# A fused cross-attention and FFN kernel: the first three row tiles projected by a W_in that is not centred, and the mask steps three tiles later

## The chip, the cores and the metric

The kernel runs on one core of one Trainium2 chip. The metric is the device time in microseconds; three runs of the kernel before gave 839.51, 840.79 and 841.10 us, median 840.79. The engines are TensorE (PE in the profile; PEld is its weight load), VectorE (DVE), ScalarE (ACT), GpSimd (POOL) and SyncE (SP, which issues most DMAs). Each works through its own queue of instructions in order and waits on semaphores.

## The reference, cut to what matters

```
x: 4096 x 512, ctx: 3202 x 1024, mask: 3202 (int32)
h    = rmsnorm(layernorm(x), g_res) @ W_in + b_in          # 512 -> 512
s    = linear scan over ctx rows of rmsnorm(ctx, g_init)[:, :512]
plug = clip(cumsum(boundary_mask) - 1, 0, 3201), where boundary_mask is 1 at cumsum(mask) - 1
x    = x + h + s[plug]
x    = x + gelu(layernorm(x) @ W1 + b1) @ W2 + b2          # 512 -> 2048 -> 512
```

All in float32. The kernel keeps this precision by splitting each factor in a high part (float32r, one pass of TensorE) and a low part, and adding three products: high by high, high by low, low by high.

The layernorm in front of W_in subtracts each row's mean and divides by a deviation; the RMS norm that follows only changes the divisor. So h is a row's scale `ra` times (x - mean) @ (g_res * W_in). Subtracting the mean of x is the same as taking from each column of g_res * W_in its mean over the 512 rows: that is the *centred* W_in of the kernel before.

## The kernel before

The 4096 rows of x are 32 tiles of 128 rows (`NT`), in groups of `TI` = 4. A first stage, about the first 122 us, makes x1 = x + h for all tiles; a second one, the rest of the span, does the FFN for 8 groups. The change touches the first stage, and there the order of work is written out by hand, one queue per engine: whatever stands in a `for t in range(NT)` loop under `if t == ...` is issued at that step, and waits where it stands.

What one tile t needs: `load_tile` (SyncE) brings it to `xa(t)`; TensorE's `transpose_first` turns it into a PSUM bank `first_bank[t % 3]`; ScalarE's `tile_high` writes h_hi; VectorE's `tile_low` subtracts it from the bank to h_lo; TensorE's `project` adds 4 x 3 matmuls into `p_bank[t % 3]`; VectorE's `tile_stats` (bn_stats, bn_aggr), or ScalarE's for the tiles of `ON_ACT`, gives mean and variance; GpSimd's `scales` turns the variances to `ra`; VectorE's `tile_add` (L1047) writes ra * bank + x.

W_in comes in four slabs of 128 rows. ScalarE scales each by g_res (win_g, L724). TensorE multiplies the raw slabs with g_wide, g_res spread over 128 columns (`sum_w_in`, L853), so that acc[3] holds the column sums in every partition. VectorE centres each slab (`centre_w_in`, L1139), ScalarE writes its high part, VectorE the low part of slabs 0 and 1 (`low_w_in`, L1144), GpSimd that of slabs 2 and 3 (L570). Only then do the projections of tiles 0, 1 and 2 run.

In the same loop VectorE works through the mask: `mask_parts` at t = 1, a product on TensorE (`mask_totals`, t = 4), `mask_positions` (5), `mask_carries` (6), `mask_places` (7), `mask_rows` (8), the one-hots `one_hots_q` (9), `one_hots_p` (10 and 14); TensorE counts with them at t = 16 (`count_positions`). These are chains of small operations of 26 to 78 elements per partition, each waiting for the one before. And two blocks of the context scan: ScalarE's `squares`, GpSimd's multiplication by g_init (L544, from t = 5, behind the wait for the last of four small loads that ScalarE issues, L739 and L740), ScalarE's `scale_rows`, VectorE's `scan_row` (L1053: t = 12, 13 for block 0, t = 15, 16 for block 1), then TensorE's `carry`: block 0 at t = 15, block 1 at t = 18 (L890, one product of band and the last scanned row into acc[3]), and `add_carry` on VectorE (L1071). GpSimd adds b_in to the first group's rows from t = 14 (L552).

## Time and profile before

| | |
|---|---|
| median of 3 runs | 840.79 us |
| the profiled execution | 838.94 us, its span 837.2 us |
| TensorE busy | 825.7 us (99%), 3770 matmuls |
| VectorE, ScalarE, GpSimd busy | 317.4, 288.0, 255.9 us |
| end of the first stage's projections | about 122 us |

The profile shows one execution. A busy time is the union of an engine's instructions; behind a group of instructions it says how long the engine was idle ahead of it and what released it. The chain of waits is followed backwards from the last instruction, at each step to what released it.

### The profile page before, as it was taken

The page shows a single profiled execution, that of the slowest core. Times are in us where ns is not written, and L with a number is a line of the kernel's source. Part 1 is how long each engine was busy: PE and PEld are TensorE (multiplying, and loading weights), DVE is VectorE, ACT ScalarE, POOL GpSimd, SP SyncE. Part 2 cuts the span into 40 slices and gives each one's busy share as a digit, 9 for nine tenths or more (in the row PEclk, how much of TensorE's full clock was granted, in tenths as well). Part 3 has the DMA queues.
Part 4 walks back from the last instruction along what each step waited for, and adds up shares of the span by engine and source line. Part 5 has one row for each costly group of instructions (what it writes and reads, how often), then busy time and mean ns, then how long its engine had stood idle before and what let it go on. Part 6 is the DMA issues. An engine that isn't in the chain of part 4 may idle for free.

```text
span 837.2 us, 10780 instructions
## 1 busy us (share of the span) xinstructions
PE 825.7 (99%) x3770; PEld 680.7 (81%) x3770; DVE 317.4 (38%) x521; ACT 288.0 (34%) x522; POOL 255.9 (31%) x236
## 2 busy tenths in 40 slices
PE   7998999999999999999999999999999999999998
PEld 5887888788888888888888888888888888888886
DVE  6899762664241333223332424142113311242112
ACT  5664336532622253223522262222222322222221
POOL 2272547950443026301631062303400250002000
PEclk9999999999999999999999999999999999999999
DMA  9868885252226022511234113302300240010001
GB/s 242 255 174 272 232 270 195 75 148 40 76 88 174 0 76 75 155 31 60 78 106 92 45 41 125 50 0 101 51 0 1 83 68 0 0 51 0 1 1 50
DMA packets 37328, 74.96 MB, mean 90 GB/s; under 512 B 6176, under 2 KB 6176, under 8 KB 35536
## 3 DMA queue, kind: packets, MB, share of 16 engines
q1 hardware_dynamic: 28324, 62.81, 23.2%
q0 software_dynamic: 4608, 8.39, 6.4%
q10 hardware_dynamic: 4368, 3.42, 1.4%
q8 instruction: 14, 0.23, 0.1%
q14 instruction: 14, 0.11, 0.0%
HBM read 47.87 MB, written 22.84 MB: 84 GB/s over the span
## 4 chain that ended last, share of the span: by engine, by line
PE 85%; POOL 4%; DVE 4%; DMA 2%; issue 1%; SPq 1%; ACT 1%; ACTq 0%; DVEq 0%; POOLq 0%
PE acc L860 14%; PE acc L858 14%; PE acc L859 14%; PE h_bank L858 13%; PE h_bank L860 13%; PE h_bank L859 13%; DMA xa_odd<-in_x_dram 2%; PE t_bank L917 2%; POOL w_lo L525 1%; POOL x_cur L623 1%; POOL cl L544 1%; POOL w_lo L531 1%; DVE h_lo L1039 1%; DVE st_a L1034 1%; SPq L348 0%
## 5 line engine op out<-in xcount | busy, mean ns | idle before, releaser
L1264 DVE TENSOR_TENSOR h_lo<-g_f,h_hi 128x512 fp32r<-128x512 f32 x128 | 99.7, 779 | 432.1 <-ACT g_f L795 427.1
L793 ACT ACTIVATE h_hi<-h_bank,b_c 128x512 fp32r<-128x512 f32 x128 | 88.1, 689 | 430.9 <-PE h_bank L860 426.0
L858 PE MATMUL h_bank<-xt_hi,w_hi 128*128 128x512 f32 x512 | 199.9, 390 | 0.6 <-POOL w_lo L525 0.6
L858 PE MATMUL acc<-w_hi,h_hi 128*128 128x512 f32 x512 | 199.8, 390 | 0.0
L860 PE MATMUL h_bank<-xt_hi,w_lo 128*128 128x512 f32 x512 | 199.3, 389 | 0.0
L859 PE MATMUL h_bank<-xt_lo,w_hi 128*128 128x512 f32 x512 | 199.3, 389 | 0.0
L860 PE MATMUL acc<-w_hi,h_lo 128*128 128x512 f32 x512 | 199.2, 389 | 0.0
L859 PE MATMUL acc<-w_lo,h_hi 128*128 128x512 f32 x512 | 199.2, 389 | 0.0
L858 PEld LDWEIGHTS h_bank<-xt_hi,w_hi 128*128 128x128 f32 x512 | 96.1, 188 | 20.7 <-issue 1.0
L860 PEld LDWEIGHTS h_bank<-xt_hi,w_lo 128*128 128x128 f32 x512 | 96.1, 188 | 20.0
L860 PEld LDWEIGHTS acc<-w_hi,h_lo 128*128 128x128 f32 x512 | 96.1, 188 | 20.0
L859 PEld LDWEIGHTS h_bank<-xt_lo,w_hi 128*128 128x128 f32 x512 | 96.1, 188 | 19.7
L859 PEld LDWEIGHTS acc<-w_lo,h_hi 128*128 128x128 f32 x512 | 96.1, 188 | 19.7
L858 PEld LDWEIGHTS acc<-w_hi,h_hi 128*128 128x128 f32 x512 | 96.1, 188 | 19.7
L795 ACT ACTIVATE g_f<-h_bank,b_c 128x512 f32<-128x512 f32 x128 | 87.4, 683 | 0.3 <-DVE h_lo L1264 0.3
L557 POOL DMA_INDIRECT x_next<-scan_table,idx x32 | 50.9, 1591 | 69.7 <-DMA scan_table<-cl 59.7
L623 POOL TENSOR_TENSOR x_cur<-x_next,b_b 128x512 f32<-128x512 f32 x32 | 45.0, 1436 | 58.7 <-DMA out_dram<-x_cur 58.4
L544 POOL TENSOR_TENSOR cl<-cl,g_init_b 128x512 f32<-128x512 f32 x24 | 31.9, 1334 | 97.7 <-ACT ch L704 91.8
L552 POOL TENSOR_TENSOR x_next<-x_next,b_in_b 128x512 f32<-128x512 f32 x32 | 45.4, 1418 | 33.5 <-DMA x_next<-x_part 30.2
L562 POOL TENSOR_SCALAR va_b<-mv_b 128x4 f32<-128x4 f32 x8 | 1.6, 197 | 175.8 <-DVE mv_b L1170 175.8
L858 PE MATMUL acc<-win_hi,h_hi 128*128 128x512 f32 x88 | 37.2, 422 | 2.1 <-DVE win_lo L1144 1.9
L860 PE MATMUL acc<-win_hi,h_lo 128*128 128x512 f32 x88 | 34.6, 393 | 0.0
(164 smaller groups left out, 689.3 us busy)
## 6 DMA issues: line engine op xcount, KB each, us to landing
out_dram<-x_cur SPq DMA_DIRECT2D x32, 256.0 KB, 2.1
x_next<-x_part SPq DMA_DIRECT2D x7, 1024.0 KB, 5.0
w_raw<-in_L_ffn_w_dram SPq DMA_DIRECT2D x6, 1024.0 KB, 9.0
scan_table<-cl SPq DMA_DIRECT2D x6, 896.0 KB
ch<-in_ctx_dram SPq DMA_DIRECT2D x20, 256.0 KB
cl<-in_ctx_dram SPq DMA_DIRECT2D x5, 1024.0 KB
xa_odd<-in_x_dram SPq DMA_DIRECT2D x16, 256.0 KB, 6.2
x_part<-xa_odd SPq DMA_DIRECT2D x16, 256.0 KB, 3.8
```

The costliest lines, as they stand in the source:

```text
L525: pool.tensor_tensor(w_lo[:, k, r], w_raw[:, k, r], w_hi[:, k, r].bitcast(F32), ALU.subtract).then_inc(w1_ready, 1)
L544: pool.tensor_tensor(rows[:, j, :], rows[:, j, :], g_init_b[:], ALU.mult).then_inc(g_scaled, 1)
L552: step(pool.tensor_tensor(x_next[:, i, :], x_next[:, i, :], b_in_b[:], ALU.add))
L557: pool.indirect_dma_start(x_next[:, i, :], None, rows, bass.IndirectOffsetOnAxis(ap=idx[:, i:i + 1].bitcast(U32), axis=0), compute_op=ALU. ...
L623: ins = pool.tensor_tensor(x_cur[:, i, :], x_next[:, i, :], b2_b[:], ALU.add)
L793: act.activation(h_hi[:, m % HB, :], h_bank[m % 2][:], ACT.Gelu, bias=b1_c[:, m:m + 1])
L795: act.activation(g_f32[:], h_bank[m % 2][:], ACT.Gelu, bias=b1_c[:, m:m + 1]).then_inc(gelu_done, 1)
L858: nc.tensor.matmul(dst, a_hi, b_hi, start=first, stop=False)
L859: nc.tensor.matmul(dst, a_hi, b_lo, start=False, stop=False)
L860: return nc.tensor.matmul(dst, a_lo, b_hi, start=False, stop=final)
L917: ins = nc.tensor.transpose(t_bank[i % 2][:, k * P:(k + 1) * P], n_rows[:, i, k * P:(k + 1) * P], ident[:])
L1264: dve.tensor_tensor(h_lo[:, m % HB, :], g_f32[:], h_hi[:, m % HB, :].bitcast(F32), ALU.subtract).then_inc(h_split, 1)
```

## The change

For tiles 0, 1 and 2 the product is taken with g_res * W_in as it is, split into `first_hi` (ScalarE) and `first_lo` (VectorE), in two places of memory that are free at this time. The part of the mean is put in on VectorE: `fix_tile` writes x + neg_sums * mean_ra into the result's rows, with neg_sums the negative column sums and mean_ra = mean * ra (GpSimd), and `tile_add` then adds ra * bank to that. The column sums come from one product with ones, of the four scaled slabs added up on GpSimd (`add_w_in`); ScalarE copies them out of the bank as neg_sums. Tile 3 is the first that uses the centred W_in; all four of its low parts are made on VectorE. Tiles 3 and 4 are summed in acc[3] and h_bank[0], which no tile used so far (`sums_bank`), so that they wait for no `tile_add`. The transpositions and high and low parts of tiles 4 and 5 move ahead of the loop. W_in's slabs 1 and 2 are loaded by ScalarE's queue, x tiles 0, 1, 2 by SyncE's. The warm-up is 10 instead of 14 transpositions. `mask_parts` and `mask_totals` are three steps later, the steps of the mask behind them two.

```diff
-WARM = 14
+WARM = 10
+RAW = 3
+        first_hi = place("first_hi", [P, K, D], F32R, offset=w_hi_at + 2 * WC * 4)
+        first_lo = place("first_lo", [P, K, D], F32R, offset=w_hi_at + 3 * WC * 4)
+        win_sum = ch[:, 0, :]
+        def sums_bank(t):
+            return {3: acc[3], 4: h_bank[0]}[t] if t in (3, 4) else p_bank[(t + 2 * (t < 3)) % 3]
# SyncE
-            for k in range(K):
+            for t, k in ((0, 0), (1, 3)):
+                sp.dma_start(xa(t), x_v[0, :, t, :]).then_inc(xa_loaded[t], 16)
                 sp.dma_start(win_raw[:, k, :], win_v[:, k, :]).then_inc(win_loaded[k], 16)
+            sp.dma_start(xa(2), x_v[0, :, 2, :]).then_inc(xa_loaded[2], 16)
# GpSimd
-            for k in (2, 3):
-                pool.wait_ge(win_hi_done, k + 1)
-                pool.tensor_tensor(win_lo[:, k, :], win_raw[:, k, :], win_hi[:, k, :].bitcast(F32),
-                                   ALU.subtract).then_inc(win_lo_late, 1)
+            def add_w_in(k):
+                pool.wait_ge(win_scaled, k + 1)
+                src = win_g[:, 0, :] if k == 1 else win_sum
+                ins = pool.tensor_tensor(win_sum, src, win_g[:, k, :], ALU.add)
...
+            def mean_scales(t0, n):
+                pool.wait_ge(ra_ready, t0 + n)
+                u = slice(t0, t0 + n)
+                pool.tensor_tensor(mean_ra[:, u], mv_a[:, u, 0], ra[:, u], ALU.mult).then_inc(mean_ra_ready, n)
+            add_w_in(1)
+            add_w_in(2)
+            add_w_in(3)
             scales(0, 2)
+            mean_scales(0, 2)
             scales(2, 2)
+            mean_scales(2, 1)
# ScalarE
-            for t in range(2):
-                act.dma_start(xa(t), x_v[0, :, t, :]).then_inc(xa_loaded[t], 16)
+            for k in (1, 2):
+                act.dma_start(win_raw[:, k, :], win_v[:, k, :]).then_inc(win_loaded[k], 16)
+            def high_first(k):
+                act.wait_ge(win_loaded[k], 16)
+                act.activation(first_hi[:, k, :], win_raw[:, k, :], ACT.Copy, scale=g_res_c[:, k:k + 1]).then_inc(first_hi_done, 1)
+            high_first(0)
             tile_high(0)
+            high_first(1)
+            scale_w_in(0)
+            scale_w_in(1)
+            tile_high(1)
+            high_first(2)
+            scale_w_in(2)
+            high_first(3)
+            scale_w_in(3)
+            tile_high(2)
+            act.wait_ge(win_summed, 1)
+            act.activation(neg_sums[:], acc[3][:], ACT.Copy, scale=-1.0).then_inc(neg_sums_made, 1)
             high_w_in(0)
-            tile_high(1)
-            high_w_in(1)
-            tile_high(2)
-            high_w_in(2)
-            high_w_in(3)
             tile_high(3)
+            for k in range(1, K):
+                high_w_in(k)
+            tile_high(4)
+            tile_high(5)
# TensorE
-            def sum_w_in(k):
-                pe.wait_ge(g_made, k + 1)
-                pe.wait_ge(win_loaded[k], 16)
-                ins = nc.tensor.matmul(acc[3][:], g_wide[:, k, :], win_raw[:, k, :], start=(k == 0), stop=(k == K - 1))
+            def sum_w_in():
+                pe.wait_ge(win_added, 1)
+                nc.tensor.matmul(acc[3][:], ones[:], win_sum, start=True, stop=True).then_inc(win_summed, 1)
             def project(t):
                 pe.wait_ge(x_lo, t + 1)
-                if t >= 3:
-                    pe.wait_ge(acc_read, t - 2)
+                if t == RAW:
+                    pe.wait_ge(neg_sums_made, 1)
+                if t >= 5:
+                    pe.wait_ge(acc_read, t - 4 if t < 8 else t - 2)
                 for k in range(K):
+                    if t == RAW:
+                        pe.wait_ge(win_lo_done, k + 1)
-                if t == 4:
+                if t == 7:
+                    pe.wait_ge(acc_read, 5)
                     mask_totals()
# VectorE
+            def fix_tile(t):
+                dve.wait_ge(mean_ra_ready, t + 1)
+                ins = dve.scalar_tensor_tensor(x1(t), neg_sums[:], mean_ra[:, t:t + 1], xa(t), ALU.mult, ALU.add)
+                fixed.append(own.inc(ins))
             def centre_w_in(k):
-                    dve.wait_ge(win_summed, 1)
+                    dve.wait_ge(neg_sums_made, 1)
-                dve.scalar_tensor_tensor(win_raw[:, k, :], acc[3][:], -1.0 / D, win_g[:, k, :], ALU.mult, ALU.add)\
+                dve.scalar_tensor_tensor(win_raw[:, k, :], neg_sums[:], 1.0 / D, win_g[:, k, :], ALU.mult, ALU.add)\
+            def low_first(k):
+                dve.wait_ge(first_hi_done, k + 1)
+                dve.scalar_tensor_tensor(first_lo[:, k, :], win_raw[:, k, :], g_res_c[:, k:k + 1],
+                                         first_hi[:, k, :].bitcast(F32), ALU.mult, ALU.subtract).then_inc(first_lo_done, 1)
+            for t in range(RAW):
+                fix_tile(t)
             for t in range(NT):
                 if t > 0:
                     tile_add(t - 1)
-                if 2 <= t < NT - 2:
+                if 4 <= t < NT - 2:
                     tile_low(t + 2)
-                if t == 1:
+                if t == 4:
                     mask_parts()
-                if t == 5:
+                if t == 7:
                     mask_positions()
```

The orders of the straight parts, as the engines get them, say the rest. VectorE from its first operation behind the memsets, before: first_bank appears as t_bank or acc, and win_raw is written over by the centred slab.

```order
L1039 TENSOR_TENSOR h_lo<-t_bank,h_hi 128x512 [waits x_hi]
L1139 SCALAR_TENSOR_TENSOR win_raw<-acc,win_g 128x512 [waits win_scaled,win_summed]
L1139 SCALAR_TENSOR_TENSOR win_raw<-acc,win_g 128x512 [waits win_scaled]
L1144 TENSOR_TENSOR win_lo<-win_raw,win_hi 128x512 [waits win_hi_done]
L1039 TENSOR_TENSOR h_lo<-t_bank,h_hi 128x512 [waits x_hi]
L1139 SCALAR_TENSOR_TENSOR win_raw<-acc,win_g 128x512 [waits win_scaled]
L1144 TENSOR_TENSOR win_lo<-win_raw,win_hi 128x512 [waits win_hi_done]
L1139 SCALAR_TENSOR_TENSOR win_raw<-acc,win_g 128x512 [waits win_scaled]
L1039 TENSOR_TENSOR h_lo<-acc,h_hi 128x512 [waits x_hi]
L1034 BN_STATS st_a<-xa_even 128x6 [waits xa_loaded0]
L1035 BN_AGGR mv_a<-st_a 128x2 [waits dve_self]
L1034 BN_STATS st_a<-xa_even 128x6 [waits xa_loaded1]
```

The same place now:

```order
L1198 SCALAR_TENSOR_TENSOR first_lo<-win_raw,g_res_c,first_hi 128x512 [waits first_hi_done]
L1082 TENSOR_TENSOR h_lo<-t_bank,h_hi 128x512 [waits x_hi]
L1198 SCALAR_TENSOR_TENSOR first_lo<-win_raw,g_res_c,first_hi 128x512 [waits first_hi_done]
L1082 TENSOR_TENSOR h_lo<-t_bank,h_hi 128x512 [waits x_hi]
L1198 SCALAR_TENSOR_TENSOR first_lo<-win_raw,g_res_c,first_hi 128x512 [waits first_hi_done]
L1077 BN_STATS st_a<-xa_even 128x6 [waits xa_loaded0]
L1078 BN_AGGR mv_a<-st_a 128x2 [waits dve_self]
L1198 SCALAR_TENSOR_TENSOR first_lo<-win_raw,g_res_c,first_hi 128x512 [waits first_hi_done]
L1077 BN_STATS st_a<-xa_even 128x6 [waits xa_loaded1]
L1078 BN_AGGR mv_a<-st_a 128x2 [waits dve_self]
L1082 TENSOR_TENSOR h_lo<-acc,h_hi 128x512 [waits x_hi]
L1077 BN_STATS st_a<-xa_even 128x6 [waits xa_loaded2]
```

The centring of W_in stood between the low parts of tiles 0 and 1; now the low parts of the uncentred slabs stand there, and statistics come before tile 2. What follows, up to the first `tile_add` (L1101), now reads:

```order
L1193 SCALAR_TENSOR_TENSOR win_raw<-neg_sums,win_g 128x512 [waits win_scaled,neg_sums_made]
L1193 SCALAR_TENSOR_TENSOR win_raw<-neg_sums,win_g 128x512 [waits win_scaled]
L1203 TENSOR_TENSOR win_lo<-win_raw,win_hi 128x512 [waits win_hi_done]
L1193 SCALAR_TENSOR_TENSOR win_raw<-neg_sums,win_g 128x512 [waits win_scaled]
L1203 TENSOR_TENSOR win_lo<-win_raw,win_hi 128x512 [waits win_hi_done]
L1082 TENSOR_TENSOR h_lo<-t_bank,h_hi 128x512 [waits x_hi]
L1193 SCALAR_TENSOR_TENSOR win_raw<-neg_sums,win_g 128x512 [waits win_scaled]
L1203 TENSOR_TENSOR win_lo<-win_raw,win_hi 128x512 [waits win_hi_done] x2
L1082 TENSOR_TENSOR h_lo<-t_bank,h_hi 128x512 [waits x_hi]
L1082 TENSOR_TENSOR h_lo<-acc,h_hi 128x512 [waits x_hi]
L1090 SCALAR_TENSOR_TENSOR x_next<-neg_sums,mean_ra,xa_even 128x512 [waits mean_ra_ready] x3
L1101 SCALAR_TENSOR_TENSOR x_next<-h_bank,ra,x_next 128x512 [waits dve_self,ra_ready,h_used]
```

All four slabs are centred and split here, the low parts of tiles 3, 4 and 5 are made, and three `fix_tile` (L1090) stand ahead of the first `tile_add`. Before, two `tile_stats` stood directly ahead of it and `mask_parts` behind it.

TensorE from behind the warm-up to the first projections, before:

```order
L853 MATMUL acc<-win_raw,g_wide 128x512 [waits win_loaded0,g_made]
L853 MATMUL acc<-win_raw,g_wide 128x512 [waits win_loaded1,g_made]
L846 MATMUL t_bank<-ident,xa_even 128x128 [waits xa_loaded0]
L846 MATMUL t_bank<-ident,xa_even 128x128 x3
L853 MATMUL acc<-win_raw,g_wide 128x512 [waits win_loaded2,g_made]
L853 MATMUL acc<-win_raw,g_wide 128x512 [waits win_loaded3,g_made]
L846 MATMUL t_bank<-ident,xa_even 128x128 [waits xa_loaded1]
L846 MATMUL t_bank<-ident,xa_even 128x128 x3
L846 MATMUL acc<-ident,xa_even 128x128 [waits xa_loaded2]
L846 MATMUL acc<-ident,xa_even 128x128 x3
L858 MATMUL acc<-win_hi,h_hi 128x512 [waits win_lo_done,x_lo]
L859 MATMUL acc<-win_lo,h_hi 128x512
```

and now, where L891 is a transposition and L900 to L902 are one slab's three matmuls of one tile:

```order
L891 MATMUL t_bank<-ident,xa_even 128x128 [waits xa_loaded0]
L891 MATMUL t_bank<-ident,xa_even 128x128 x3
L900 MATMUL h_bank<-first_hi,h_hi 128x512 [waits first_lo_done,x_lo]
L901 MATMUL h_bank<-first_lo,h_hi 128x512
L902 MATMUL h_bank<-first_hi,h_lo 128x512
L891 MATMUL t_bank<-ident,xa_even 128x128 [waits xa_loaded1]
L891 MATMUL t_bank<-ident,xa_even 128x128 x3
L900 MATMUL h_bank<-first_hi,h_hi 128x512 [waits first_lo_done,x_lo]
L901 MATMUL h_bank<-first_lo,h_hi 128x512
L902 MATMUL h_bank<-first_hi,h_lo 128x512
L900 MATMUL acc<-first_hi,h_hi 128x512 [waits first_lo_done,x_lo]
L901 MATMUL acc<-first_lo,h_hi 128x512
```

The first product now stands between the transpositions of tiles 0 and 1; the sum product (now one) has moved behind the products of tiles 0 and 1.

## Rows read from the trace of the kernel before

**Rows 1.** The page: busy time of each engine, its share, instructions.
```profile
PE 825.7 (99%) x3770; PEld 680.7 (81%) x3770; DVE 317.4 (38%) x521; ACT 288.0 (34%) x522; POOL 255.9 (31%) x236
```
**Rows 2.** TensorE's waits, whole span: us in total, times, longest.
```profile
PE acc L890 <- DVE cl_next L1053: 2.1, 1, 2.1
```
**Rows 3.** Chain of waits in order of time: start, us, what.
```profile
73.32 1.66 DVE cl_next L1053
...
75.11 1.10 PE acc L890 x2
76.20 0.23 PE acc L858
```
**Rows 4.** Windows: length; busy and instructions by engine; granted clock, DMA share, GB/s.
```profile
5.40:9.65 4.25, 4.25 (x14) 2.18 (x13) 0.01 (x1) 3.60 (x7) 0.00 (x0) 1.00 1.03 374
...
21.62:74.96 53.34, 51.16 (x279) 41.88 (x277) 49.27 (x98) 34.72 (x86) 25.36 (x29) 1.00 0.73 218
```
**Rows 5.** VectorE's waits from 21.6 to 75 us.
```profile
DVE h_lo L1039 <- ACT h_hi L686: 1.4, 3, 0.8
DVE xa_even L1047 <- POOL ra L520: 0.4, 1, 0.4
```
**Rows 6.** Timeline of VectorE, set-up: start, us, instruction, idle before and releaser.
```profile
9.65 0.69 DVE L1039 TENSOR_TENSOR h_lo<-t_bank,h_hi 128x512 fp32r<-128x512 f32 x1 [4.25 <-ACT h_hi L686]
10.26 1.28 DVE L1139 SCALAR_TENSOR_TENSOR win_raw<-acc,win_g 128x512 f32<-128x512 f32 x2
...
15.25 0.69 DVE L1034 BATCH_NORM_STATS2 st_a<-xa_even 128x6 f32<-128x512 f32 x1
...
16.14 0.66 DVE L1034 BATCH_NORM_STATS2 st_a<-xa_even 128x6 f32<-128x512 f32 x1
...
18.37 0.69 DVE L1039 TENSOR_TENSOR h_lo<-t_bank,h_hi 128x512 fp32r<-128x512 f32 x1 [1.29 <-ACT h_hi L686]
```
**Rows 7.** Timeline of TensorE, set-up.
```profile
2.53 3.25 PE L886 MATMUL acc<-ident 128*128 128x128 f32 x14 [2.53 <-POOL iota_p L504]
5.57 2.15 PE L853 MATMUL acc<-win_raw,g_wide 128*128 128x512 f32 x4
7.56 0.60 PE L846 MATMUL t_bank<-ident,xa_even 128*128 128x128 f32 x4
8.00 1.88 PE L853 MATMUL acc<-win_raw,g_wide 128*128 128x512 f32 x4
...
12.48 0.47 PE L858 MATMUL acc<-win_hi,h_hi 128*128 128x512 f32 x1 [1.73 <-DVE win_lo L1144]
```
**Rows 8.** Timeline of VectorE and of GpSimd, mask steps and scans.
```profile
35.06 1.28 DVE L1100 TENSOR_TENSOR ib<-cum_f,ia 128x26 int32<-128x26 f32 x1
...
36.59 0.19 DVE L1102 TENSOR_TENSOR ic<-cum_f,ia 128x26 int32<-128x26 f32 x1
...
43.02 1.27 DVE L1079 TENSOR_SCALAR ib<-ia 128x26 int32<-128x26 int32 x1
...
59.63 1.41 DVE L1053 SCALAR_TENSOR_TENSOR cl<-cl 128x512 f32<-128x512 f32 x2
...
72.27 2.69 DVE L1053 SCALAR_TENSOR_TENSOR cl_next<-cl_next 128x512 f32<-128x512 f32 x2
...
35.02 1.29 POOL L544 TENSOR_TENSOR cl<-cl,g_init_b 128x512 f32<-128x512 f32 x1
...
61.18 1.28 POOL L552 TENSOR_TENSOR x_next<-x_next,b_in_b 128x512 f32<-128x512 f32 x1
...
71.44 4.66 POOL L552 TENSOR_TENSOR x_next<-x_next,b_in_b 128x512 f32<-128x512 f32 x3
```
**Rows 9.** Timeline: ScalarE's issue of the last small load, GpSimd's wait for it.
```profile
19.09 0.46 ACTq L740 DMA_DIRECT2D b_c<-in_L_ffn_b_dram  x1
...
33.70 2.61 POOL L544 TENSOR_TENSOR cl<-cl,g_init_b 128x512 f32<-128x512 f32 x2 [3.76 <-DMA b_c<-in_L_ffn_b_dram]
```
**Rows 10.** SyncE's issues of the W_in slabs, and line L340's time to landing.
```profile
0.82 1.83 SPq L340 DMA_DIRECT2D win_raw<-in_L_xattn_W_in_dram  x4
...
DMA to landing us min/median/max: 3.6/4.7/6.2
```

More of the change, by code:

```diff
@@ L202, in xattn_ffn @@
         ident = sb("ident", [P, P])
-        g_wide = early("g_wide", [P, K, P])
+        neg_sums = early("neg_sums", [P, D])
         tri = early("tri", [P, P])
@@ L407, in _ @@
             sp.sem_inc(table_stored, STORED)
-            for t in range(2, 8):
+            for t in range(3, 8):
                 load_tile(t)
@@ L719, in _, with scale_w_in @@
             act.wait_ge(g_res_loaded, 16)
-            for k in range(K):
-                act.activation(g_wide[:, k, :], ones[:], ACT.Copy, scale=g_res_c[:, k:k + 1]).then_inc(g_made, 1)
-            for k in range(K):
+            def high_first(k):
                 act.wait_ge(win_loaded[k], 16)
+                act.activation(first_hi[:, k, :], win_raw[:, k, :], ACT.Copy, scale=g_res_c[:, k:k + 1]).then_inc(first_hi_done, 1)
+            def scale_w_in(k):
                 act.activation(win_g[:, k, :], win_raw[:, k, :], ACT.Copy, scale=g_res_c[:, k:k + 1]).then_inc(win_scaled, 1)
@@ L1046, in tile_add @@
                 u = t % XR
-                dve.scalar_tensor_tensor(x1(t), p_bank[t % 3][:], ra[:, u:u + 1], xa(t), ALU.mult, ALU.add).then_inc(acc_read, 1)
+                if t < RAW:
+                    dve.wait_ge(dve_self, fixed[t])
+                rows = x1(t) if t < RAW else xa(t)
+                dve.scalar_tensor_tensor(x1(t), sums_bank(t)[:], ra[:, u:u + 1], rows, ALU.mult, ALU.add).then_inc(acc_read, 1)
             def scan_row(b, rows, j):
@@ L1183, in transposed_low @@
                                   xt_hi[:, :, i * P:(i + 1) * P].bitcast(F32), ALU.subtract).then_inc(t_lo, 1)
+            low_first(0)
             tile_low(0)
+            low_first(1)
+            tile_low(1)
+            low_first(2)
+            tile_stats(0)
+            low_first(3)
+            tile_stats(1)
+            tile_low(2)
+            tile_stats(2)
+            tile_stats(3)
             centre_w_in(0)
@@ L1188, in _ @@
             low_w_in(0)
[L1189 removed]
             centre_w_in(2)
             low_w_in(1)
+            tile_low(3)
             centre_w_in(3)
[L1193 to L1198 removed]
+            low_w_in(2)
+            low_w_in(3)
+            tile_low(4)
+            tile_low(5)
+            for t in range(RAW):
+                fix_tile(t)
             for t in range(NT):
```

76 lines of the change are left out of this document (36 added, 40 removed).

## The prediction, made before the change was run

> **What bounds the kernel now.** I read the page's engine totals first: TensorE is busy 825.7 of 837.2 us [rows 1]. Its idle time is 11.5 us, so no change off its path can bring more than that, and the next view is TensorE's list of waits. Beside the start-up it has one long entry, 2.1 us ahead of a matmul on acc, released by VectorE's cl_next (L1053) [rows 2]; the timeline adds 1.73 us ahead of the first projection at 12.48, released by win_lo [rows 7].
>
> The question is what ends each of the two. The chain of waits, read in order of time, arrives at 75.11 us on TensorE (`carry(1)`) from VectorE: the two scans of block 1 end at 74.98 us [rows 3]. So everything TensorE saved ahead of 75.11 us would be returned there, unless VectorE's scan ends sooner. Behind it the chain runs on in TensorE's own matmuls, 0.23 us each. I therefore read VectorE by windows [rows 4]: idle for all of 5.40 to 9.65, and from 21.62 (its first `tile_add`) to 74.96 it is busy 49.27 of 53.34. Most of the missing 4 us are gaps of 0.03 to 0.1 us inside chains of small operations. Waits for others are only 1.4 + 0.4 us [rows 5]. VectorE's queue, not TensorE's, sets when `carry(1)` can start: the change is to be priced on VectorE.
>
> **The change on TensorE.** Four sum products of two records each go (2.15 and 1.88 us from 5.57 on, with a transposition between), one comes back; the first projection no longer waits at 12.48 for the centred weights [rows 7]. By the same rows: ten warm-up transpositions end at about 4.8 us, transposition 0 at 5.6, and the first product starts once first_lo and h_lo are there, about 7.4. Each step of a tile's projection is three matmuls at 0.23 us [rows 3], 0.7 us. Going down the new order I get tile 3 finished at about 23 us with transposition 5 done, where the old one has it at 25.4 with one transposition fewer. That is 2.5 to 3 us won, all ahead of 75 us, so it counts for nothing unless VectorE follows. Tiles 3 and 4 in idle banks take two `acc_read` waits away that do not appear in TensorE's list: nothing. The DMAs: x tiles 0, 1, 2 and W_in 0, 3 on SyncE's queue, W_in 1, 2 on ScalarE's; the same seven loads of 256 KB, in another order. The last W_in slab landed at 8.4 us (the slowest landing, 6.2, from the last issue at 2.2 [rows 10]), and first_hi(3) will not be asked for before 10.5; nothing.
>
> **The change on VectorE.** Operations of 128x512 follow each other at 0.60 us (9.65 to 10.26), a `tile_stats` costs 0.89 (15.25 to 16.14) [rows 6].
> - Added: four `low_first`, two `low_w_in` that GpSimd did, three `fix_tile`: 9 x 0.60 = 5.4 us.
> - Idle that goes: 4.25 us ahead of the first h_lo and 1.29 ahead of h_lo(3) [rows 6], and the 1.8 of [rows 5], since VectorE is later than its suppliers there: -7.3 us.
> - Idle that comes. W_in 0 is now second on its queue, landing where the second slab did, some 5.4 us (issue 1.3, landing 3.6 to 4.7 [rows 10]); first_hi takes 0.70, so `low_first(0)` starts at about 6.1: 0.7 us after the memsets. h_lo(1) needs transposition 1, which TensorE issues behind `project_raw(0, 0)`: h_lo(0) ends at 7.4, three matmuls 8.2, transposition 8.8, h_hi 9.4; VectorE has only `low_first(1)` to fill with: 1.5 us idle. h_lo(2) needs transposition 2, behind `project_raw(1, 2)`, done at about 13.7, h_hi at 14.3: 0.8 us. The sums: matmul done at 16.0, neg_sums 16.6, just as the statistics end, so almost nothing; two waits for win_hi in the centring chain of 0.15 each. `low_first(3)` meets GpSimd's `add_w_in(2)`, 0.4 (below). Sum 3.9 us, first `tile_add` at about 25.4 instead of 21.62.
> Net: 5.4 + 3.9 - 7.3 = +2.0 us at the scan's end. The statistics of tile 4, moved behind the adds, are the same work. Between ends: with W_in 0 at 4.4 (as the first slab) and both tile waits 0.4 shorter it is +0.2; with landings 1 us later, +3.2.
>
> **Mask steps and GpSimd.** They add no instruction; what they cost hangs on whom they meet. The 26-element operation at 35.06 takes 1.28 us, its sister at 36.59 0.19; GpSimd's multiplication ran from 35.02 for 1.29, and both end together. The same at 43.02 (1.27). The two scans take 1.41 us at 59.63 but 2.69 at 72.27, beside three GpSimd additions that also stretch [rows 8]. So a VectorE operation with its operands in SBUF waits for a GpSimd tensor_tensor and the other way round. The price in the old order is 1.1 + 1.1 us in the mask steps, 1.3 at the scans.
> The Trainium skill's page "SBUF — State Buffer", section "SBUF: two separate sides", says the port pair of VectorE and GpSimd is an exclusive lock held for the whole instruction, and that a VectorE operation with two SBUF inputs takes part. The trace agrees (1.28 against 0.19). By that rule this change has more to lose than its operation counts say: `centre_w_in` and `fix_tile` now read neg_sums from SBUF instead of a bank, and would block wherever GpSimd runs.
> In the new order GpSimd's multiplications by g_init wait for the last of the small loads (b1_c, issued at 19.09, GpSimd idle 3.8 us for it until 33.7 [rows 9]). ScalarE issues these behind h_hi(5), about 4.3 us later, so GpSimd starts at 36 to 38 us instead of 33.7 and then runs without pause for four to six operations of 1.29, under `mask_positions` (38), `mask_carries` (41) and `mask_places` (45). I count three to five meetings of 0.5 to 1.2 us, against 2.2 us in these steps before. The scans of block 0, free of it in the old order, then come at 63, together with the first addition of b_in (61.2 before [rows 8], and later by the statistics that its queue waits for): one more, about 1 us. All told -2 at best, +3 at worst; I take +1.2, since GpSimd's share of the stretch rises and no step becomes free of it. `add(8)` needs ra of tiles 8 to 11, at 41 to 43.5, and is due at 44: no wait.
>
> **Sum.** +2.0 + 1.2 = +3.2 us at `carry(1)`; behind it nothing changes order, so the end moves by as much. The profiled execution took 838.94 us (span 837.2) and would take 842.1. The median of the three runs shown is 840.79, 1.85 above it; on that scale the forecast is 844.0 us.
>
> **Rivals.**
 In the old order TensorE goes on with sum products; in the new one it pauses 1.8 us before its first product and again before tile 1. If the slow level lasts to about 13 us, six projection steps and a transposition cost double: 6 x 0.7 + 0.4 = 4.6 us, of which VectorE's chain feels about 4 through neg_sums. 847 to 849 us. For it: four warm-up steps fewer. Against: the old order has a 1.73 us pause at 10.75 and comes back fast.
> The skill's page "TensorE: Matmul & The Clock Gate", section on the clock gate, says idling brings the 1.2 GHz level back and that where in a run the switch falls varies; by the rule the +4 us is possible, and may come in some runs only.
> (b) No measurable change. Only the queue sum counts, the meetings cancel or fall, the loads land early: 0 to +1.5 us, 841 to 842. What a measurement here can tell from no change is 0.2%, 1.7 us.
> (c) Faster. The mask steps fall between GpSimd's operations, the 2.2 us of stretching in them go, and the new idle is at its low end: +0.2 - 2.2 = -2.0, about 839 us. It decides if the scan of block 1 ends before 74.96 us; then TensorE's head start of 3 us is worth something. For it: the 3 us are really there. Against: VectorE gets 5.4 us more work, and no part of its work goes.
>
> **How the numbers follow.** Forecast 0.47 (own range +1.7 to +5 us), (a) 0.13, (b) 0.26, (c) 0.14. Slower by over 0.2% is the forecast and (a), 0.60; within 0.2% is (b), 0.26; faster (c), 0.14. The range leaves out most of (c) and the upper part of (a): 840.3 to 847.5.
>
> **What would show it.** Right: VectorE's first `tile_add` at 25 to 26 us, its queue without waits from there to the scan at 76 to 79 us; tile 3's projection finished at 22 to 24 us; TensorE idle 5 us or more between 55 and 79 us (at count_positions for the one-hots and at `carry(1)`), more than before by what it won; two or more mask operations of over 1 us beside GpSimd's. Wrong: the first `tile_add` before 24 us, or the scan ended before 75 us, or a TensorE wait at `carry(1)` no longer than 2.1 us. If the early products start 0.46 us apart instead of 0.23, it is (a).

## The result and the profile after

The median of after is 846.67 us (841.85 to 848.15, 14 runs), that of before on the same chip 841.00 (839.12 to 842.91, 14 runs). The ratio is 1.0058 with a 95% interval of 1.0047 to 1.0070, about +4.9 us (the medians alone differ by 5.7; both kernels' times lie in groups). The forecast was +3.2 us, with 840.3 to 847.5 as its range.

One caution for every number below. The runs of after gather in two places, three at 841.9 to 842.7 and eleven at 845.5 to 848.2; those of before do too, three at 839.1 to 839.5 and eleven at 840.6 to 842.9. The profiled execution of after (847.73 us, span 846.0) is of the upper group, that of before (838.94, span 837.2) of the lower. Their difference, 8.8 us, is therefore larger than the usual one.

The page's totals of after, columns as in [rows 1]:

```profile
PE 828.4 (98%) x3760; PEld 681.8 (81%) x3760; DVE 326.8 (39%) x530; ACT 289.6 (34%) x523; POOL 258.5 (31%) x239
```

TensorE is busy for 2.7 us more though it has ten records fewer, and VectorE for 9.4 us more with nine instructions more. Nine operations at 0.60 us are 5.4, so about 4 us of VectorE's time are stretching. TensorE's waits from 20 us on (us in total, times, longest), which stand against [rows 2]:

```profile
PE acc L933 <- DVE cl L1107: 4.6, 1, 4.6
PE acc L900 <- DVE h_lo L1082: 2.5, 4, 1.2
```

The long wait has moved from `carry(1)` (cl_next, 2.1 us) to `carry(0)` (cl, 4.6 us). VectorE in the same stretch waits for nobody. Its timeline (start, us, instruction, idle before and releaser), set-up first, which answers to [rows 6]:

```profile
6.76 0.75 DVE L1198 SCALAR_TENSOR_TENSOR first_lo<-win_raw,g_res_c,first_hi 128x512 fp32r<-128x512 f32 x1 [1.36 <-ACT first_hi L755]
...
11.34 0.69 DVE L1082 TENSOR_TENSOR h_lo<-t_bank,h_hi 128x512 fp32r<-128x512 f32 x1 [2.56 <-ACT h_hi L718]
...
16.96 0.69 DVE L1082 TENSOR_TENSOR h_lo<-acc,h_hi 128x512 fp32r<-128x512 f32 x1 [1.64 <-ACT h_hi L718]
...
26.32 2.07 DVE L1090 SCALAR_TENSOR_TENSOR x_next<-neg_sums,mean_ra,xa_even 128x512 f32<-128x512 f32 x3
28.30 0.75 DVE L1101 SCALAR_TENSOR_TENSOR x_next<-h_bank,ra,x_next 128x512 f32<-128x512 f32 x1
```

The first `tile_add` starts at 28.30 instead of 21.62; forecast was 25.4. Of the 2.9 us beyond it 0.65 is first_lo (6.76 against 6.1: W_in 0, issued at 1.3, took 4.6 us to land, at 5.9 and not 5.4), and the rest comes through h_lo(1) and h_lo(2), 1.9 and 2.7 us later than forecast. TensorE's timeline says why; it answers to [rows 7]:

```profile
8.17 0.80 PE L900 MATMUL h_bank<-first_hi,h_hi 128*128 128x512 f32 x1 [1.98 <-DVE h_lo L1082]
8.76 0.63 PE L901 MATMUL h_bank<-first_lo,h_hi 128*128 128x512 f32 x1
9.19 0.63 PE L902 MATMUL h_bank<-first_hi,h_lo 128*128 128x512 f32 x1
...
13.85 0.39 PE L901 MATMUL acc<-first_lo,h_hi 128*128 128x512 f32 x1
14.08 0.39 PE L902 MATMUL acc<-first_hi,h_lo 128*128 128x512 f32 x1
```

The first projection products are 0.43 us apart (8.76 to 9.19), the later ones 0.23 (13.85 to 14.08), and the four transpositions at 9.61 take 1.05 us instead of 0.60.
```profile
2.50:13.50 11.00, 8.71 (x27) 6.43 (x28) 6.59 (x9) 7.23 (x12) 3.28 (x6) 1.00 1.00 301
...
28.30:83.56 55.26, 47.82 (x244) 37.97 (x243) 52.88 (x98) 31.09 (x79) 24.53 (x28) 0.94 0.58 164
```

From its first `tile_add` to the end of the scan of block 1 VectorE now has 55.26 us (53.34 before) and is busy for 52.88 of them (49.27 before), with the same 98 instructions. So the instructions themselves have become longer. VectorE's mask steps and scans, against [rows 8]:

```profile
34.43 1.49 DVE L1133 TENSOR_SCALAR part_i<-mask_i 128x26 int32<-128x26 int32 x2
...
35.96 1.24 DVE L1141 CAST part_f<-part_i 128x78 f32<-128x78 int32 x1
...
45.82 1.26 DVE L1131 TENSOR_SCALAR ia<-ib 128x26 int32<-128x26 int32 x1
...
51.44 1.28 DVE L1169 TENSOR_SCALAR ia<-fa 128x26 int32<-128x26 f32 x1
...
54.92 1.00 DVE L1133 TENSOR_SCALAR ib<-ia 128x26 int32<-128x26 int32 x1
...
64.09 1.78 DVE L1107 SCALAR_TENSOR_TENSOR cl<-cl 128x512 f32<-128x512 f32 x1
...
68.08 2.36 DVE L1107 SCALAR_TENSOR_TENSOR cl<-cl 128x512 f32<-128x512 f32 x2
...
80.86 2.70 DVE L1107 SCALAR_TENSOR_TENSOR cl_next<-cl_next 128x512 f32<-128x512 f32 x2
```

And GpSimd's work at those times (L559 is the multiplication by g_init, L567 the addition of b_in):

```profile
34.59 2.56 POOL L559 TENSOR_TENSOR cl<-cl,g_init_b 128x512 f32<-128x512 f32 x2
...
45.75 1.29 POOL L559 TENSOR_TENSOR cl<-cl,g_init_b 128x512 f32<-128x512 f32 x1
54.59 1.30 POOL L559 TENSOR_TENSOR cl_next<-cl_next,g_init_b 128x512 f32<-128x512 f32 x1 [1.90 <-ACT ch_next L736]
...
62.66 2.66 POOL L559 TENSOR_TENSOR cl_next<-cl_next,g_init_b 128x512 f32<-128x512 f32 x1
...
67.89 1.27 POOL L567 TENSOR_TENSOR x_next<-x_next,b_in_b 128x512 f32<-128x512 f32 x1
```

Each long mask operation ends with a multiplication of GpSimd: 45.82 + 1.26 = 47.08 and 45.75 + 1.29 = 47.04, and so at 54.92 (a further one runs from 51.39). The first scan of block 0 (64.09) meets a multiplication too, the pair at 68.08 the addition of b_in. Against the unstretched time (0.18 to 0.2 us for the small ones, 0.70 for a scan operation) the excess is 1.10 and 1.04 in `mask_parts`, 1.08, 1.10, 0.82 behind it, 1.10 and 0.95 in the scans of block 0: 7.2 us in all. Before, the same sum is 2.8 us (1.1 + 1.1 of [rows 8] and 0.6 in smaller pieces). So meetings cost +4.4 us. The old idle that went (1.8, [rows 5]) and about 0.3 us less of other work (two low parts fewer, one `tile_stats` more) stand against that: +2.3 us. Measured is 55.26 - 53.34 = +1.9; the other 0.4 us are not accounted for.

TensorE meanwhile: `carry(0)` in before, then `carry(0)` and `carry(1)` in after, and two windows of after.

```profile
61.60 1.02 PE L890 MATMUL acc<-cl,band 128*128 128x512 f32 x2
```

```profile
70.58 2.05 PE L933 MATMUL acc<-cl,band 128*128 128x512 f32 x2 [4.59 <-DVE cl L1107]
...
84.02 1.02 PE L933 MATMUL acc<-cl_next,band 128*128 128x512 f32 x2
```

```profile
60.00:70.00 10.00, 5.99 (x31) 4.74 (x29) 9.72 (x13) 2.15 (x4) 7.13 (x8) 0.92 0.67 178
70.00:80.00 10.00, 9.42 (x55) 7.08 (x56) 9.76 (x16) 5.22 (x14) 1.16 (x2) 0.74 0.85 229
```

TensorE has no head start here. It finishes tile 3 at 26.1 us (25.4 before), waits for low parts of VectorE on the way, and is at `carry(0)` at 70.58 - 4.59 = 65.99 us, where before it was at 61.60. Around the 4.6 us wait the granted clock falls to 0.92 and then 0.74 (a mixture of both levels), and `carry(0)` takes 2.05 us for what takes 1.02 at 84.02. With that TensorE reached `carry(1)` 0.46 us after the scan ended, without a wait there. Whether it alone, or VectorE alone, would have been as late in this execution is not separated.

The book of the profiled pair: the scan of block 1 ends at 83.56 us against 74.96, +8.6 (first `tile_add` +6.7, then +1.9), and the span is 8.8 longer. The span is 762.2 us after the scan's end in before, 762.4 in after. That relation is a tool for the experiments: in six of the seven that leave the carries where they are, the scan of block 1 ends 762.1 to 762.3 us before the end of the span, and 763.8 in the seventh, e3_three_more, whose granted clock is 0.83 in the 10 us behind it.

### The profile page after: what moved, and what is told of

Same layout as the page of the kernel before. It is cut to its first block, busy times and chain, and to the rows that moved or that the text cites. A ratio compares the mean times of both kernels' runs of the same rounds, so it can differ in the third digit from the quotient of the medians.

```text
span 846.0 us, 10774 instructions
## 1 busy us (share of the span) xinstructions
PE 828.4 (98%) x3760; PEld 681.8 (81%) x3760; DVE 326.8 (39%) x530; ACT 289.6 (34%) x523; POOL 258.5 (31%) x239
## 2 busy tenths in 40 slices
DMA packets 37328, 74.96 MB, mean 89 GB/s; under 512 B 6176, under 2 KB 6176, under 8 KB 35536
## 4 chain that ended last, share of the span: by engine, by line
PE 87%; DVE 6%; POOL 4%; issue 1%; ACT 1%; DMA 1%; SPq 0%; DVEq 0%; POOLq 0%; ACTq 0%
PE acc L900 14%; PE acc L902 14%; PE acc L901 14%; PE h_bank L900 14%; PE h_bank L902 13%; PE h_bank L901 13%; PE t_bank L960 2%; POOL w_lo L540 1%; DVE h_lo L1082 1%; DVE st_a L1077 1%; POOL x_cur L655 1%; POOL cl L559 1%; PE t_bank L891 1%; POOL w_lo L546 1%; DMA win_raw<-in_L_xattn_W_in_dram 1%
## 5 line engine op out<-in xcount | busy, mean ns | idle before, releaser
L900 PE MATMUL h_bank<-xt_hi,w_hi 128*128 128x512 f32 x512 | 199.9, 390 | 0.6 <-POOL w_lo L540 0.6
L900 PE MATMUL acc<-w_hi,h_hi 128*128 128x512 f32 x512 | 199.8, 390 | 0.0
L902 PE MATMUL h_bank<-xt_hi,w_lo 128*128 128x512 f32 x512 | 199.3, 389 | 0.0
L902 PE MATMUL acc<-w_hi,h_lo 128*128 128x512 f32 x512 | 199.2, 389 | 0.0
L900 PEld LDWEIGHTS h_bank<-xt_hi,w_hi 128*128 128x128 f32 x512 | 96.1, 188 | 20.7 <-issue 1.0
L902 PEld LDWEIGHTS acc<-w_hi,h_lo 128*128 128x128 f32 x512 | 96.1, 188 | 20.0
L902 PEld LDWEIGHTS h_bank<-xt_hi,w_lo 128*128 128x128 f32 x512 | 96.1, 188 | 20.0
L900 PEld LDWEIGHTS acc<-w_hi,h_hi 128*128 128x128 f32 x512 | 96.1, 188 | 19.7
L559 POOL TENSOR_TENSOR cl<-cl,g_init_b 128x512 f32<-128x512 f32 x24 | 31.9, 1336 | 94.6 <-ACT ch L736 91.6
L567 POOL TENSOR_TENSOR x_next<-x_next,b_in_b 128x512 f32<-128x512 f32 x32 | 45.4, 1417 | 32.5 <-DMA x_next<-x_part 29.2
L900 PE MATMUL acc<-win_hi,h_hi 128*128 128x512 f32 x76 | 33.1, 436 | 2.5 <-DVE h_lo L1082 2.5
L748 ACT ACTIVATE xt_hi<-t_bank 128x512 fp32r<-128x512 f32 x32 | 17.4, 596 | 47.0 <-PE h_bank L902 37.4
```

Source lines behind the costliest of these rows:

```text
L559: pool.tensor_tensor(rows[:, j, :], rows[:, j, :], g_init_b[:], ALU.mult).then_inc(g_scaled, 1)
L567: step(pool.tensor_tensor(x_next[:, i, :], x_next[:, i, :], b_in_b[:], ALU.add))
L748: act.activation(xt_hi[:, :, i * P:(i + 1) * P], t_bank[i % 2][:].rearrange("p (k r) -> p k r", k=K), ACT.Copy).then_inc(t_hi, 1)
L900: nc.tensor.matmul(dst, a_hi, b_hi, start=first, stop=False)
L902: return nc.tensor.matmul(dst, a_lo, b_hi, start=False, stop=final)
```

## The experiments

Theory A was: the set-up puts VectorE's queue back (more operations, slow TensorE clock), meetings with GpSimd put it back further, and the end of its scan of block 1 is the end of the kernel. Theory B differed from case to case and is quoted with each. "Ratio" is to before, timed beside it.

### The slow clock

```diff
             transpose_first(0)
+            warm_up(10)
             project_raw(0, 0)
```

> The change, with ten more transpositions of the constant between the transposition of tile 0 and the first product, so that TensorE does not pause there. Theory A (the slow level of TensorE's clock lasts past the first products because it paused 1.98 us ahead of them, and VectorE's neg_sums come late by it): products 0.23 us apart from the first one or the second on, neg_sums at about 16.5 instead of 18.58 us, the first tile_add at 25.5 to 26.5 instead of 28.30, the end 2 to 3 us earlier than the changed kernel (843.5 to 844.5), and no longer two clusters of times. Rival B (VectorE's queue alone is the cost, the clock does not matter since its products are only waited for by an idle VectorE): the end within 1 us of the changed kernel, 846 to 847.5.

Measured: 843.37 us (841.48 to 847.77, 8 runs), ratio 1.0040 (1.0022 to 1.0059). TensorE's timeline of this kernel:

```profile
8.17 0.50 PE L900 MATMUL h_bank<-first_hi,h_hi 128*128 128x512 f32 x1 [0.45 <-DVE h_lo L1083]
8.51 0.39 PE L901 MATMUL h_bank<-first_lo,h_hi 128*128 128x512 f32 x1
```

The same products at the same 8.17 us, but now at the full rate: the third follows at 8.74, 0.23 behind the second. VectorE, and then GpSimd's first multiplications:

```profile
26.48 0.74 DVE L1102 SCALAR_TENSOR_TENSOR x_next<-h_bank,ra,x_next 128x512 f32<-128x512 f32 x1
...
42.07 1.25 DVE L1132 TENSOR_SCALAR ia<-ib 128x26 int32<-128x26 int32 x1
...
75.16 2.70 DVE L1108 SCALAR_TENSOR_TENSOR cl_next<-cl_next 128x512 f32<-128x512 f32 x2
```

```profile
34.78 2.55 POOL L559 TENSOR_TENSOR cl<-cl,g_init_b 128x512 f32<-128x512 f32 x2 [1.96 <-DMA b_c<-in_L_ffn_b_dram]
```

The first `tile_add` comes 1.8 us earlier: that is the clock's price in the set-up. But the scan ends at 77.86, 5.7 us earlier, because only one mask operation is still held for long: GpSimd's first multiplications wait for the last small load and start where they did in after (34.78 and 34.59), while VectorE's steps come 1.8 us sooner and fall ahead of them and between the next ones. Clock and meetings are not separate costs. In the traces A holds. In the times it is less sure: the fillers bring 3.3 us by the medians, but 1.5 by the ratios (1.0058 less 1.0040), whose intervals overlap, and the traced executions are one of after's upper and one of e1_fill's lower times. A also said that there would be no two clusters, and the runs still spread over 6 us, so a slow start in some executions is not all that separates the groups.

### The mask steps alone

```diff
# in before: mask_parts, mask_totals and the product of totals 3 steps later, the rest 2
-                if t == 1:
+                if t == 4:
-                if t == 5:
+                if t == 7:
```

> The kernel before, with the mask steps alone moved as in the change (parts and totals three steps later, the others two), nothing else. Theory A (the mask steps now meet GpSimd's multiplications and the scans meet them more often): VectorE's scan of block 1 ends 1 to 3 us later than 74.98, the end is at 842 to 844. Rival B (where the mask steps stand does not matter, they meet GpSimd as often as before): within 0.8 us of the kernel before, 841.0.

Measured: 841.11 us (840.69 to 841.57, 12 runs), ratio 1.0007 (0.9998 to 1.0017): nothing by the median. The rows show mostly an exchange:

```profile
33.20 0.69 DVE L1039 TENSOR_TENSOR h_lo<-t_bank,h_hi 128x512 fp32r<-128x512 f32 x1 [2.76 <-ACT h_hi L686]
...
41.24 1.26 DVE L1077 TENSOR_SCALAR cum_i<-ic 128x26 int32<-128x26 int32 x1
...
61.28 2.34 DVE L1053 SCALAR_TENSOR_TENSOR cl<-cl 128x512 f32<-128x512 f32 x2
```

One meeting fewer in the mask steps, and two new ones in the scans of block 0 (the first takes 1.77 us at 57.29), which had been free [rows 8]: 0.5 us more in all. The scan of block 1 nevertheless ends at 76.76, 1.8 us later than in before's profile, which is what A said of it; most of that is the wait of 2.76 us at 33.20, behind a load of an x tile for which ScalarE waited 4.19 us (2.63 before). In time B holds: the later steps by themselves are no measurable cause. All twelve runs lie where the upper group of before lies; of the 25 runs of before beside them, eight are at 839.1 to 839.4. Whether that load makes the two groups was not tried.

### More work ahead of the first tile_add

```diff
# in before; each tile_add of tiles 0 to 2 also waits for its own operation here
...
+            for t in range(3):
+                dve.wait_ge(ra_ready, t + 1)
+                ins = dve.scalar_tensor_tensor(x1(t), win_g[:, 0, :], ra[:, t:t + 1], xa(t), ALU.mult, ALU.add)
...
```

> The kernel before, with three more VectorE operations of 128x512 (results overwritten by the tile_adds) ahead of the first tile_add, at the place of the change's fix_tile. Theory A (VectorE's queue up to the scan of block 1 sets the end): first tile_add 1.8 us later, the scan of block 1 0 to 1.8 us later since the 1.8 us of waits behind it may take part of it up, the end at 841.5 to 843. Rival B (TensorE sets the end and VectorE has room): no difference, 841.0 within 0.4.

Measured: 843.64 us (843.41 to 845.07, 6 runs), ratio 1.0038 (1.0025 to 1.0051), +2.6 by medians.

```profile
21.61 1.38 DVE L1204 SCALAR_TENSOR_TENSOR x_next<-win_g,ra,xa_even 128x512 f32<-128x512 f32 x2
23.58 0.75 DVE L1204 SCALAR_TENSOR_TENSOR x_next<-win_g,ra,xa_even 128x512 f32<-128x512 f32 x1 [0.59 <-POOL ra L520]
25.17 0.75 DVE L1049 SCALAR_TENSOR_TENSOR x_next<-acc,ra,xa_even 128x512 f32<-128x512 f32 x1
```

Three operations cost 2.6 us here, since one waits 0.59 for ra. This execution had a slow start too (four sum products 3.37 us, against 2.15 in [rows 7]), another 0.9. The scan of block 1 ends at 79.49, 4.5 us later than before. A has the direction, but the time is beyond its 841.5 to 843: the end went back by more than the 1.8 us of the operations alone.

### After without fix_tile

```diff
-                rows = x1(t) if t < RAW else xa(t)
+                rows = xa(t)
...
-            for t in range(RAW):
-                fix_tile(t)
```

The mean's part of tiles 0 to 2 is left out.

> The change without its three fix_tile operations (the part of the mean of tiles 0 to 2 is left out of the result). Theory A (VectorE's queue): the first tile_add and the scan of block 1 about 2 us earlier, as much as the three take (2.07 us), the end at 844.5 to 845. Rival B (another engine, say TensorE's late start at the slow clock, sets the end): less than 0.5 us.

Measured: 841.95 us (841.21 to 845.76, 12 runs), ratio 1.0024 (1.0012 to 1.0036). That is 4.7 us below after by the medians and 2.9 by the ratios, for operations of 2.07 us.

```profile
25.36 0.74 DVE L1099 SCALAR_TENSOR_TENSOR x_next<-h_bank,ra,xa_even 128x512 f32<-128x512 f32 x1
```

```profile
8.12 0.50 PE L900 MATMUL h_bank<-first_hi,h_hi 128*128 128x512 f32 x1 [2.02 <-DVE h_lo L1082]
...
10.01 0.63 PE L902 MATMUL h_bank<-first_hi,h_lo 128*128 128x512 f32 x1
```

2.94 us earlier than in after: the operations, and 0.9 because TensorE was slow for less long. Behind a pause of 2.02 us, as long as in after, its first products ran at the full rate here; only from 9.6 to 12.8 us they were 0.43 apart. From the first `tile_add` to the scan's end it is 51.86 us against 55.26: again the meetings changed with the shift. A's direction, and more than it said.

### GpSimd's multiplications taken away

```diff
-                pool.tensor_tensor(rows[:, j, :], rows[:, j, :], g_init_b[:], ALU.mult).then_inc(g_scaled, 1)
+                if isinstance(b, int) and b < NA:
+                    pool.tensor_tensor(spare[:, R * b + j, :], neg_half[:], neg_half[:], ALU.mult).then_inc(g_scaled, 1)
...
```

The eight multiplications of blocks 0 and 1 become operations of four elements; the factor g_init is left out.

> The change, with GpSimd's eight multiplications of the context rows by g_init in blocks 0 and 1 left out (an operation of four elements stands for each; the result lacks that factor there). Theory A (VectorE's mask steps and scans wait for these 1.29 us operations of GpSimd, and that, more than its longer queue, is what the change costs): none of the small VectorE operations takes over 0.4 us, the scan of block 1 ends 48.5 to 50.5 us behind the first tile_add instead of 55.3, the end at 840 to 842, 5 to 6 us faster than the changed kernel. Rival B (the queue sum alone): the mask steps go on stretching or the end moves by less than 2 us, 845 to 847.

Measured: 840.45 us (839.13 to 841.80, 12 runs), ratio 0.9988 (0.9976 to 1.0000).

```profile
34.72 0.40 DVE L1137 TENSOR_SCALAR part_i<-mask_i 128x26 int32<-128x26 int32 x2
...
62.09 2.37 DVE L1111 SCALAR_TENSOR_TENSOR cl<-cl 128x512 f32<-128x512 f32 x2
...
74.88 2.69 DVE L1111 SCALAR_TENSOR_TENSOR cl_next<-cl_next 128x512 f32<-128x512 f32 x2
```

The set-up is as slow as in after (first `tile_add` at 28.60), all VectorE's instructions are there, and from it to the scan's end it is 48.97 us instead of 55.26. No small operation takes over 0.4 us (the row at 34.72 is two). The one meeting of block 0 that stays is that with the addition of b_in, 2.37 us at 62.09. By the rows of after, multiplications held VectorE for 7.2 - 0.95 = 6.2 us; the profile is 6.3 shorter in this stretch, the medians 6.2 and the ratios 5.9. This settles the mechanism, and its size in the changed kernel. With these meetings gone the kernel is 0.12% below before, although VectorE starts its tiles 7 us later. That is not like against like: before has 2.8 us of such meetings of its own, and no run takes them from it. What the change would cost without them in both kernels is not measured.

### Low parts of slabs 2 and 3 back on GpSimd

```diff
+            low_late(2)     # GpSimd: win_lo = win_raw - win_hi
+            low_late(3)
-            low_w_in(2)     # VectorE
-            low_w_in(3)
```

> The change, with the low parts of the centred W_in's slabs 2 and 3 back on GpSimd (ahead of it idle from 21 to 33 us). Theory A (VectorE's queue sets the end, each operation of 128x512 ahead of the first tile_add costs at least its 0.6 us): first tile_add about 1.2 us earlier, the end 1.2 to 4 us earlier, the more the fewer mask steps meet GpSimd, 842.5 to 845.5. Rival B (GpSimd's two operations of 1.29 us block VectorE's fix_tile and h_lo beside them): first tile_add no earlier, the end unchanged, 846 to 847.

Measured: 847.67 us (843.08 to 848.37, 7 runs), ratio 1.0061 (1.0039 to 1.0084): no gain. VectorE and then GpSimd:

```profile
22.32 1.45 DVE L1205 SCALAR_TENSOR_TENSOR win_raw<-neg_sums,win_g 128x512 f32<-128x512 f32 x1
```

```profile
21.94 1.28 POOL L597 TENSOR_TENSOR win_lo<-win_raw,win_hi 128x512 fp32r<-128x512 f32 x1 [1.29 <-ACT win_hi L771]
```

The centring of the next slab waits out GpSimd's operation (1.45 instead of 0.7), and h_lo waits as well (1.18 us). The first `tile_add` is at 28.14, 0.16 earlier. So taking the low parts off VectorE wins nothing, as B said: on GpSimd they hold VectorE instead.

### mask_parts two steps earlier

```diff
-                if t == 4:
+                if t == 2:
                     mask_parts()
```

> The change with one step moved: mask_parts at t = 2 instead of 4 on VectorE (28 to 33 us, while GpSimd is idle from 21.3 to 33.3). Theory A (two of the change's meetings, 34.43 and 35.96, are this step beside GpSimd's first multiplication, and each loses 1.1 us): mask_parts takes 1.7 us, the scan of block 1 ends 2 to 3 us earlier, the end at 843.5 to 845.0, with the slow clock at the start still in it. Rival B (the meetings only move to the next steps, since GpSimd's multiplications move with the statistics): less than 1 us, 846 to 847.

Measured: 845.73 us (845.41 to 847.41, 6 runs), ratio 1.0063 (1.0044 to 1.0082); 0.9 us below after by the medians, no lower by the ratio. The two meetings are gone (the first of them now takes 0.39 us at 29.07), and the scan ends at 81.85, 1.7 earlier. Of this 0.75 arose ahead of the first `tile_add` (27.55), where nothing was changed: TensorE rose to its full rate at 12.1 us in this execution. Behind it VectorE now waits for others (the longest 0.8 us, for TensorE), and TensorE for h_lo:

```profile
PE acc L900 <- DVE h_lo L1082: 4.0, 2, 3.3
```

The time lies between A's range and B's; the rows are closer to B: small operations put ahead of low parts that TensorE waits for delay TensorE's tiles, and these VectorE.

### The later carries

In before, and in after with the fillers, `carry(0)`, `count_positions` and `carry(1)` stand one tile later, with what reads them:

```diff
-                if t == 15:
+                if t == 16:      # carry(0)
-                if t == 16:
+                if t == 17:      # count_positions
-                if t == 18:
+                if t == 19:      # carry(1)
```

> The kernel before, with the three products that wait for VectorE each one tile later on TensorE (carry 0 at t = 16, count_positions at 17, carry 1 at 19) and their readers on VectorE likewise. Theory A (TensorE's 2.1 us at carry 1 are a wait for VectorE's place in its queue, and TensorE has a tile ready to put there): the wait shrinks to under 1 us, the scan stays where it is or ends earlier by the moved add_carry, the end at 838.5 to 840, 1 to 2 us faster than before. Rival B (TensorE meets the same queue one tile later through h_lo): no difference, 841 within 0.6.

Measured in before: **838.46 us** (837.34 to 839.16, 9 runs), ratio 0.9960 (0.9946 to 0.9974), which beats both kernels. Its waits for VectorE:

```profile
PE acc L858 <- DVE h_lo L1039: 0.9, 2, 0.7
...
PE acc L890 <- DVE cl L1071: 0.6, 1, 0.6
```

The wait at `carry(1)` of [rows 2] is gone, though VectorE's scan ends later (75.93 against 74.96): TensorE had a tile's products left to do in its place.

> e1_fill (the change, TensorE kept busy ahead of the first product) with the three products of e5_before_later one tile later. Theory A (TensorE has won some 3 us by then and returns them at the carries): waits at the carries under 2 us together, the end 2 to 3 us ahead of e1_fill's 843.4, 840 to 841.5. Rival B (it waits for h_lo in VectorE's queue instead): 843 to 844.

Measured in after with fillers: 840.12 us (839.51 to 844.56, 12 runs), ratio 0.9991 (0.9975 to 1.0007), 3.2 below the same kernel with the old carries. TensorE's waits:

```profile
PE acc L900 <- DVE h_lo L1083: 3.2, 4, 1.2
...
PE acc L933 <- DVE cl L1126: 1.6, 1, 1.6
PE t_bank L960 <- DVE n_rows L1237: 1.5, 1, 1.5
```

It doesn't reach e5_before_later. The waits point at the reason: VectorE's queue, longer by the change's operations, holds TensorE up at h_lo and n_rows instead.

> e8_fill_later with mask_parts at t = 2 as well. Theory A (VectorE's queue, less the meetings): 837.5 to 839.5, as fast as or faster than e5_before_later's 838.5. Rival B (what is left is TensorE's waits for h_lo ahead of the mask steps, which an earlier mask_parts makes longer): 840 to 841.

With `mask_parts` at step 2 as well: 842.92 us (842.42 to 843.90, 12 runs), ratio 1.0025 (1.0012 to 1.0038), 2.8 worse than without that move. TensorE's h_lo waits are 4.7 us in total, the longest 3.3. My theory missed; rival B had the reason, though the time lies 2 us above its range as well.

## Why the prediction was right, and where not

Direction, time and range were right, and so was the main step: VectorE's queue up to the scan of block 1 sets the end. All kernels with the old carries but e3_three_more show it by the constant 762 us behind that scan, and e6_no_multiplication shows it from the side: an edit on GpSimd alone, off the chain, moved the end by about 6 us. TensorE's head start of 2.5 to 3 us was said to be worth nothing; in fact it did not come. Tile 3 was finished at 26.1 us instead of 22 to 24, and TensorE was at `carry(0)` 4.4 us later than before, behind slow first products and waits for VectorE's low parts. Tiles 3 and 4 in idle banks and the order of the loads left no trace. Some luck was in it: the sum was too small in both of its uncertain terms, and profile against profile the difference at the scan is +8.6 us, outside the sum's own range of +1.7 to +5. By their sizes:

- **Added work, 5.4 us.** Right. e3_three_more and e4_no_fix price three of the nine operations at 2.6 (with a wait of 0.59) and 2.07 us.
- **New idle, 3.9 us** (the items listed add up to 3.7). Too small, and this is the first failed term. The three waits ahead of first_lo, h_lo(1) and h_lo(2) were forecast as 0.7, 1.5 and 0.8 us and took 1.36, 2.56 and 1.64. I let the products follow each other at 0.23 us from 7.4 us on. They ran at 0.43 to 13.5. I had this as rival (a), with about 4 us in the place of the forecast; it came together with it, at about 2.3 us in the profile and 1.8 in the experiment. It should have been a term of the sum, at part of its price, and not a case of its own. The first slab's landing, 0.65 us late at first_lo, is the other part of the miss.
- **Meetings, +1.2 us.** The second failed term: +4.4 in the profiled execution, above my worst of +3. The lock itself was read rightly from [rows 8]. The Trainium skill's page "SBUF — State Buffer", section "SBUF: two separate sides", which calls the shared port an exclusive lock, is borne out by e6_no_multiplication, and what it says of VectorE operations with two SBUF inputs by the centring with neg_sums, 1.45 us beside GpSimd's operation in e7_lows_gpsimd. What failed was the count: I took three to five meetings at their mean excess, and did not see that a chain of small operations that follows a shift can hit a multiplication at every step.
- **When GpSimd starts.** Wrong. I had the multiplications wait for the last small load until 36 to 38 us. They started at 34.59, behind its ra at 33.61; the load was there. I had its issue 4.3 us later and moved the landing by as much. The issue came 6.3 us later (25.35 against 19.09), but the load then landed within 9.2 us instead of the 14.6 of [rows 9], and in e1_fill, e4_no_fix and e7_lows_gpsimd GpSimd's wait for it ended at 34.3 to 35.1. So they ran right under `mask_parts` at 34.43, which the prediction did not have.
- **Where TensorE waits.** 5 us or more between 55 and 79 were forecast, and 4.6 came, ending at 70.58, but at `carry(0)`, not at `count_positions` and `carry(1)`. I had not priced the scans of block 0 with both their meetings (64.09, 68.08). Behind that wait the granted clock fell, so that no wait at `carry(1)` was left; by the prediction's own list this counted against it, yet the reason was TensorE's clock and not an earlier VectorE.
- **Rival (c)** asked for a scan ended before 74.96 us. No kernel with the change's new operations had that; the earliest were 76.61 (e8_fill_later), 77.22 (e4_no_fix, with six of the nine new operations) and 77.57, with GpSimd's multiplications taken away.

Together: the usual difference of +4.9 us is 1.7 above the +3.2 forecast, and the profiled +8.6 at the scan is the forecast 3.2, 2.9 more in the set-up (6.7 instead of 3.8) and 2.5 more behind it (meetings 3.2 more, the rest 0.7 less). The two groups of after's times are not fully explained. The fillers show that the moment at which TensorE gets its full rate shifts the mask steps against GpSimd's, and that such a shift is worth 5.7 us between profiled executions (e1_fill against after, at the scan's end); but only one execution of each kernel is traced, and what separates the two groups of before stays open.

## What to carry to other kernels

When a change shifts one engine's queue against another's and both share a port, price the meetings at the new phase: list the partner's operations with their starts and lay the shifted ones over them; here a shift of 1.8 us changed them by 3.9 us (e1_fill). When the busiest engine waits for another's queue, put other ready work in the place of the wait: moving the waiting product (`carry`) one tile later gained 0.4%. Taking work off the waiting engine and giving more to the one that it waits for did not pay: the re-ordered set-up lost 0.6%.
